# Attention, feed-forward and top-k on one core: the last query group's residual rows and second product in freed buffers, under a planner with new numbers

## The chip, the cores and the metric

One core of a Trainium2 chip. The number is device time in microseconds for the whole kernel; lower is better. TensorE is called PE here, VectorE DVE, ScalarE ACT, GpSimd POOL, and SyncE, which issues the DMAs, SP.

## The reference

`x` has shape (2, 4096, 256), float32. With C = 256:

```python
qkv = x @ w_attn + b_attn; q, k, v = split(qkv)
attn = softmax(q @ k.T / sqrt(C) + causal_mask)          # 4096 x 4096 per batch
x = layernorm(x + (attn @ v) @ w_proj + b_proj)
scores = x @ w_router;  top = top_k(scores, 3072)        # per batch of 4096 rows
y = x; y[top] = gelu(x[top] @ w_block)
out = layernorm(x + y)
```

## The kernel before

**Tiling.** The 4096 rows of a batch are cut into 8 groups of 512 queries, so there are 16 groups G = 0..15; G = 15 is the last. For each group the kernel goes over the key tiles of 128 rows that the mask leaves: 4 tiles on the diagonal (512, 384, 256 and 128 queries wide) and 4g full ones, 32 tiles for G = 15. Two tiles that follow each other are one softmax *unit* (128x1024); a diagonal tile is a unit by itself. Products are made with float32 halves: each is three matmuls (high by high, high by low, low by high).

**Steps of a group.** `scores` puts one tile's first product into one of two banks `sbank` (6 matmuls, L535), ACT copies it to a ring (L955), DVE keeps the running maximum (L992, L997). `row_max` transposes the maximum on PE (L1030), DVE reduces it (L1040 to L1047), PE spreads it again (L1053). Only then can the group's softmax begin: `softmax z` subtracts the maximum on DVE (L1066), `softmax exp` on ACT (L1073), `softmax hi` rounds to the high half on ACT (L1080; three buffers `parts`, so that unit u waits for PE to have finished unit u-3), `softmax lo` makes the low half on DVE (L1085). `values` is the second product, accumulated over all tiles of the group in two banks `obank` (L1134 to L1136, 6 matmuls of 512 columns for a full tile); its tiles of v come by DMA into six buffers (L1103). The first values tile of a group waits until the group before has been copied out of `obank` by ACT (`attention_out ot`, L1194, into `ot_sb`).

**After the second product.** PE turns the sums (L1225), DVE divides and adds the residual row `r` (`attention_out evac`, L1240, L1244), takes the statistics (L1251, L1256), POOL makes the root (`istd`, L1155 to L1160), ACT normalises (L1343). `r` is `xres[:, G % 2]`: rows of x loaded by SP (`attention_out load`, L1177) once the group two before has left that buffer, the bias added on POOL (`residual`, L1186). For G = 15 the router's product of these rows is taken ahead, on DVE (`last router`, L1373). The block product and gelu follow (`ffn`, L1477, L1542), the top-k search on DVE with counts on PE (`search`, L1668 to L1704; PE L1724), and the choice between the two outcomes (`final pick`, L1917). The last groups' work on ACT for both outcomes is `final own` and `final sums` (L1902, L1907), on rows that SP reloads during G = 15 (L1850, L1851).

**Order.** No engine's order is written by hand. Every step is put into a named stream of its engine; the function `merged` lists the waits and costs of each, `urgency` the longest way from it to the end, and `planned` walks through time and picks, engine by engine, the startable step with the smallest time rounded by `MARGIN_US`, then the largest urgency plus `PREFER_US`. `COSTS` and a few constants give its durations. The order it makes is what each engine executes, and an engine that waits for one step lets nothing behind it pass.

## Time and profile before

| | us |
|---|---|
| runs of the kernel | 958.93, 961.22, 964.9; median 961.22 |
| span of the profiled execution | 962.9 |
| PE busy in it | 934.3 |
| DVE / ACT / POOL busy | 791.0 / 637.6 / 303.6 |
| DMA queue 1, share of 16 engines | 51.5% |

The profiled execution has no other time than its span, which is 1.7 us above the median of the runs. Busy time of PE counts a matmul from its start to its modelled end, and matmuls overlap, so a full row of busy time still says nothing of the pace: that is read from the distance between two starts.

### The profile page before, as it was taken

The numbers are of one execution on the slowest core, as the hardware profiler recorded it, in microseconds if no ns is written. First come the engines' busy times: TensorE is split into PE (matmuls) and PEld (weight loads), VectorE is DVE, ScalarE is ACT, GpSimd is POOL, SyncE is SP. The second block draws the span as 40 slices with busy tenths as digits, with TensorE's granted clock in tenths as the row PEclk, the third lists the DMA queues.
The fourth block names the chain that finished last, engine by engine and source line by source line (L and its number), as shares of the span: only waits on it lengthen the run. The fifth ranks groups of instructions, "written<-read, shape, count | busy, mean of one in ns | idle before, by whom it ended". The sixth has DMA issues, their size and how long they took to land.

```text
span 962.9 us, 15643 instructions
## 1 busy us (share of the span) xinstructions
PE 934.3 (97%) x5018; PEld 799.2 (83%) x5018; DVE 791.0 (82%) x1494; ACT 637.6 (66%) x1009; POOL 303.6 (32%) x460
## 2 busy tenths in 40 slices
PE   9999999999999999999999999999999999998892
PEld 7889988888888888888889998888888888887671
DVE  5789886967976885699989898999899789489768
ACT  4467665764873776486757757586689577449794
POOL 3423231333220335414541253314212422131162
PEclk9999999999999999999999999999999999999996
DMA  6535344454364365488533633535769635347734
GB/s 212 166 114 171 113 141 122 120 158 126 101 184 116 102 187 155 132 255 277 175 109 94 199 108 110 164 102 172 247 223 295 212 106 153 99 144 241 264 128 175
DMA packets 89044, 155.84 MB, mean 162 GB/s; under 512 B 8442, under 2 KB 18300, under 8 KB 88964
## 3 DMA queue, kind: packets, MB, share of 16 engines
q1 hardware_dynamic: 88964, 154.85, 51.5%
q8 instruction: 41, 0.67, 0.3%
q14 instruction: 39, 0.32, 0.1%
HBM read 114.96 MB, written 39.86 MB: 161 GB/s over the span
## 4 chain that ended last, share of the span: by engine, by line
PE 93%; DVE 3%; DMA 1%; ACT 1%; issue 1%; DVEq 0%; POOL 0%; SPq 0%; ACTq 0%
PE sbank L535 38%; PE fbank L535 13%; PE obank L1134 11%; PE obank L1136 11%; PE obank L1135 10%; PE obank L1128 2%; PE obank L1130 2%; PE obank L1129 2%; DMA vs<-v_scratch 1%; PE fbank L1225 1%; PE mbank L1053 1%; PE mbank L1030 1%; DVE tail L1917 1%; PE fbank L1490 1%; DMA xraw<-xt 0%
## 5 line engine op out<-in xcount | busy, mean ns | idle before, releaser
L535 PE MATMUL sbank<-qT,xT 128*128 128x512 f32 (+2 forms) x1728 | 411.5, 378 | 0.2 <-issue 0.2
L535 PEld LDWEIGHTS sbank<-qT,xT 128*128 128x128 f32 x1728 | 304.9, 188 | 52.8 <-issue 0.6
L955 ACT COPY ring<-sbank 128x512 f32<-128x512 f32 (+3 forms) x286 | 156.2, 548 | 179.4 <-PE sbank L535 132.0
L1085 DVE TENSOR_TENSOR ring_lo<-ring,parts 128x1024 fp32r<-128x1024 f32 (+4 forms) x175 | 174.4, 1007 | 21.9 <-ACT parts L1080 21.3
L1134 PE MATMUL obank<-ring_lo,vs 128*128 128x512 f32 x476 | 182.5, 383 | 7.4 <-issue 3.5
L1136 PE MATMUL obank<-parts,vs 128*128 128x512 f32 x480 | 183.2, 382 | 0.0
L1135 PE MATMUL obank<-parts,vs 128*128 128x512 f32 x480 | 182.9, 381 | 0.0
L1080 ACT CAST parts<-ring 128x1024 fp32r<-128x1024 f32 (+4 forms) x175 | 144.8, 834 | 45.5 <-PE obank L1136 35.8
L1066 DVE TENSOR_TENSOR ring<-ring,mbank 128x1024 f32<-128x1024 f32 (+4 forms) x175 | 158.2, 944 | 7.3 <-PE mbank L1053 7.2
L1073 ACT ACTIVATE ring<-ring 128x1024 f32<-128x1024 f32 (+4 forms) x175 | 142.6, 842 | 21.6 <-DVE ring L1066 21.2
L997 DVE TENSOR_TENSOR runmax<-ring,runmax 128x1024 f32<-128x1024 f32 x84 | 106.6, 1269 | 59.3 <-ACT ring L955 58.6
L1134 PEld LDWEIGHTS obank<-ring_lo,vs 128*128 128x128 f32 x476 | 90.4, 190 | 25.1 <-issue 6.7
L1556 POOL TENSOR_TENSOR yb<-xres,yb 128x512 f32<-128x512 f32 x28 | 41.0, 1481 | 210.6 <-ACT yb L1542 80.1
L1136 PEld LDWEIGHTS obank<-parts,vs 128*128 128x128 f32 x480 | 90.9, 189 | 17.0
L1135 PEld LDWEIGHTS obank<-parts,vs 128*128 128x128 f32 x480 | 91.2, 190 | 16.1
L1186 POOL TENSOR_TENSOR xres<-xres,b_tot 128x512 f32<-128x512 f32 x32 | 49.0, 1554 | 67.5 <-DMA xres<-x 66.1
L839 POOL TENSOR_TENSOR xT<-xraw,xT 128x512 fp32r<-128x512 f32 x27 | 38.4, 1436 | 78.0 <-ACT xT L821 77.0
L1452 POOL TENSOR_TENSOR ot_sb<-ot_sb,yb 128x512 f32<-128x512 f32 x16 | 22.5, 1405 | 98.5 <-PE fbank L1225 80.6
L992 DVE TENSOR_TENSOR runmax<-ring,runmax 128x512 f32<-128x512 f32 (+3 forms) x74 | 44.9, 606 | 9.7 <-ACT ring L955 8.5
L535 PEld LDWEIGHTS fbank<-WV,xT 128*128 128x128 f32 x384 | 49.8, 191 | 2.3 <-issue 0.3
L535 PE MATMUL fbank<-WV,xT 128*128 128x256 f32 x384 | 51.2, 283 | 0.0
L535 PE MATMUL fbank<-xT,A 128*128 128x512 f32 x192 | 49.4, 393 | 0.2 <-POOL xT L839 0.2
(244 smaller groups left out, 1257.7 us busy)
## 6 DMA issues: line engine op xcount, KB each, us to landing
vs<-v_scratch SPq DMA_DIRECT2D x288, 256.0 KB, 2.9
v_scratch<-vnew SPq DMA_DIRECT2D x30, 512.0 KB, 3.1
xres<-x SPq DMA_DIRECT2D x16, 512.0 KB, 4.0
out<-tail SPq DMA_DIRECT2D x32, 256.0 KB, 2.8
x_scratch<-xres SPq DMA_DIRECT2D x14, 512.0 KB, 3.0
y_scratch<-yb SPq DMA_DIRECT2D x14, 512.0 KB, 4.1
tail<-x_scratch SPq DMA_DIRECT2D x28, 256.0 KB, 3.4
tail<-y_scratch SPq DMA_DIRECT2D x28, 256.0 KB, 4.0
```

The costliest lines, as they stand in the source:

```text
L535: mm = eng.matmul(o, lhs(lh, k), rhs(rh, k), start=n == 0, stop=n == len(todo) - 1)
L955: act.copy(slot(n)[:, c0:], sbank[n % NSS][:, c0:]).then_inc(a_copy, 1)
L992: dve.tensor_tensor(runmax[:, 0, c0:], slot(n)[:, c0:], runmax[:, 0, c0:], ALU.max).then_inc(v_max, 1)
L997: dve.tensor_tensor(runmax[:, :, :], slots(ns, 0), runmax[:, :, :], ALU.max).then_inc(v_max, 1)
L1066: dve.tensor_tensor(slots(ns, c0), slots(ns, c0), mbank[:, None, c0:].broadcast_to([P, len(ns), GQ - c0]), ALU.subtract).then_inc(v_z, 1)
L1073: act.activation(slots(ns, c0), slots(ns, c0), ACT.Exp, scale=SCALE).then_inc(a_exp, 1)
L1080: act.copy(hi_of(u), slots(ns, c0)).then_inc(a_hi, 1)
L1085: dve.tensor_tensor(slots_lo(ns, c0), slots(ns, c0), f32(hi_of(u)), ALU.subtract).then_inc(v_lo, 1)
L1134: pe.matmul(o, vh, lo_, start=i == 0, stop=False)
L1135: pe.matmul(o, vh, hi_, start=False, stop=False)
L1136: mm = pe.matmul(o, vl, hi_, start=False, stop=last)
L1186: pool.tensor_tensor(r[:, 2 * j:2 * j + 2], r[:, 2 * j:2 * j + 2], b_tot[:, None, :].broadcast_to([P, 2, C]), ALU.add).then_inc(g_xres, 1)
```

## The change

Four things are changed.

1. Rows of x for G = 15 are loaded into the end of `tail`, which is another name for the memory of x^T (`xT`), as soon as the last scores tile and the last projection are done (`p_s >= n_tiles` and the fill of v). Before, they went to `xres[:, 1]` and waited for group 13 to leave it.
2. The second product of G = 15 is accumulated in the two score banks `sbank`, not in `obank`, so its first tile waits for the last scores copy (`a_copy`), not for the copy of group 14. The banks of the late block products and of a small product (`last_ow`, now in `mbank`) are dealt anew.
3. `COSTS` and small per-instruction terms are set anew; a term is added that makes PE's operations cost 1.85 times as much for 3.5 us after it has been idle for over 1.3 us.
4. `PREFER_US` and `MARGIN_US` are replaced as a whole (by tables of 61 and 49 entries).

```diff
 COLD_US, COLD, COLD_STREAMS = 4.0, 1.85, ()
+IDLE_US, SLOW_US = 1.3, 3.5
...
-PREFER_US = {"ffn flo": 100, "final load": 100, "project vhi": 100, "ffn store": 100, "last chain": 60,
...
+PREFER_US = {"final_roots own": 462, "last": 416, "project qlo": 324, "project vhi": 309, "scores copy": 267,
...
-COSTS = {"pe": (.0, 1 / 2400, .2), "act": (.13, 1 / 1200, .14), "dve": (.09, 1 / 960, .12),
-         "pool": (.35, 1 / 460, .1), "sp": (.45, 0.0, 0.0)}
+COSTS = {"pe": (.0, 1 / 2383, .2), "act": (.075, 1 / 1200, .17), "dve": (.065, 1 / 960, .13),
+         "pool": (.1, 1 / 445, .18), "sp": (.45, 0.0, 0.0)}
...
-        time = r.time * (COLD if n in COLD_STREAMS or e == "pe" and when < COLD_US else 1.0)
+        if e == "pe" and when > 2 * COLD_US and when - free[e] > IDLE_US:
+            slow = when + SLOW_US
+        time = r.time * (COLD if n in COLD_STREAMS or e == "pe" and when < slow else 1.0)
...
-        bank_no[f] = (3, 4, 5, 3, 4, 5, 6, 3)[4 * (G - LATE) + 2 * j + (kind == "ff")]
+        bank_no[f] = (5, 6, 5, 3, 4, 5, 6, 3)[4 * (G - LATE) + 2 * j + (kind == "ff")]
...
-                if bank_no[f] == 6:
-                    eng.wait_ge(v_ot, CC)
-                    eng.wait_ge(v_ow, 1)
-                elif bank_no[f] == 5:
-                    eng.wait_ge(v_ot, 1)
+                if bank_no[f] >= 5:
+                    eng.wait_ge(a_ot, CC * (turned(LATE) + 1))
                 elif bank_no[f] >= 3:
-                    eng.wait_ge(a_copy, n_tiles)
+                    eng.wait_ge(v_ot, bank_no[f] - 2)
...
-        last_ow = obank[1][:, 0:QT]
+        last_ow = mbank[:, 160:160 + QT]
+
+        summed = lambda G: sbank if G == len(groups) - 1 else obank
...
                 if i == 0:
-                    if G and straight(G - 1):
+                    if G == len(groups) - 1:
+                        pe.wait_ge(a_copy, n_tiles)
+                    elif G and straight(G - 1):
                         pe.wait_ge(v_h, QT * G)
...
-                    o = obank[c][:, c0:]
+                    o = summed(G)[c][:, c0:]
...
             r = xres[:, G % 2]
+            if G == len(groups) - 1:
+                r = flat[:, (NUT - 2) * 512:NUT * 512].rearrange("p (t c) -> p t c", t=QT)
...
             def load(sp):
-                if G >= 2:
+                if G == len(groups) - 1:
+
+                    sp.wait_ge(p_s, n_tiles)
+                    filled(sp, ("v", G, 1))
+                elif G >= 2:
                     sp.wait_ge(st_x1[G % 2], 16 * (G // 2))
...
-                dve.tensor_copy(ot_sb[:, c, :], obank[c][:, :]).then_inc(v_ot, 1)
+                dve.tensor_copy(ot_sb[:, c, :], summed(G)[c][:, :]).then_inc(v_ot, 1)
```

The number of instructions on each engine stays the same; their order changes in every group. Three places in G = 15 follow. In the order lists the name left of the arrow is written, those right of it are read.

**PE, from the transpose of the last maximum to its spreading.** Before, the transpose is followed by the first half of group 13's block product (`fbank<-WB`, twelve matmuls, of which three rows are shown):

```order
L1136 MATMUL obank<-parts,vs 128x512
L1030 MATMUL mbank<-ident,runmax 128x128 x4
L535 MATMUL fbank<-WB,vnew_b 128x256 x2
L535 MATMUL fbank<-WB,x1p 128x256
...
L1053 MATMUL mbank<-ident,mcol 128x128 x4
```

Now it stands one values tile of group 14 earlier, and that tile comes after it:

```order
L1151 MATMUL obank<-parts,vs 128x512
L1043 MATMUL mbank<-ident,runmax 128x128 x4
L1149 MATMUL obank<-ring_lo,vs 128x512
L1150 MATMUL obank<-parts,vs 128x512
...
L1066 MATMUL mbank<-ident,mcol 128x128 x4
```

Two values tiles stood between the last projection and the transpose, now one; the block product's halves come after the spreading, the second one after the diagonal tiles of G = 15.

**DVE, the four router products of G = 15.** Before, they stand after fifteen units have had their z and ten their lo, behind the first evacuation of group 14:

```order
L1244 SCALAR_TENSOR_TENSOR xres<-fbank,rsum,xres 128x256 x2
L1066 TENSOR_TENSOR ring<-ring,mbank 128x1024
L1251 BN_STATS bnst<-xres 128x6 x2
L1085 TENSOR_TENSOR ring_lo<-ring,parts 128x1024
L1373 ISA runmax,mcol<-xres,wr 128x256
...
L1085 TENSOR_TENSOR ring_lo<-ring,parts 128x1024 x3
L1240 RECIPROCAL rsum<-fbank 128x2
```

Now three of them stand ahead of the first full lo, the fourth two lo's later, and they read `tail`:

```order
L1079 TENSOR_TENSOR ring<-ring,mbank 128x1024
L1098 TENSOR_TENSOR ring_lo<-ring,parts 128x128
L1394 ISA runmax,mcol<-tail,wr 128x256
...
L1098 TENSOR_TENSOR ring_lo<-ring,parts 128x1024 x2
L1394 ISA runmax,mcol<-tail,wr 128x256
L1394 ISA mcol 128x1
L1079 TENSOR_TENSOR ring<-ring,mbank 128x1024
```

**PE, the last values tiles and what follows.** Before, all values tiles are done before the first late transpose (`ident,tail`), the first three counts of the search (`cmp,ones_bf`) and the turn of G = 15 (`ident,ot_sb`):

```order
L1134 MATMUL obank<-late_lo,vs 128x512
L1135 MATMUL obank<-parts,vs 128x512
L1136 MATMUL obank<-parts,vs 128x512
L1490 MATMUL sbank<-ident,tail 128x128 x4
L1724 MATMUL fbank<-cmp,ones_bf 128x120 x3
L1225 MATMUL fbank<-ident,ot_sb 128x128 x8
```

Now the three counts stand ahead of the last seven values tiles, in the middle of a unit:

```order
L1745 MATMUL fbank<-cmp,ones_bf 128x120 x3
L1149 MATMUL sbank<-ring_lo,vs 128x512
...
L1149 MATMUL sbank<-late_lo,vs 128x512
L1150 MATMUL sbank<-parts,vs 128x512
L1151 MATMUL sbank<-parts,vs 128x512
L1511 MATMUL obank<-ident,tail 128x128 x4
L1246 MATMUL fbank<-ident,ot_sb 128x128 x8
```

What moved is the counts; the late transpose still stands ahead of the turn.

## Rows read from the trace of the kernel before

**Rows 1.** The page's head.

```profile
span 962.9 us, 15643 instructions
```

**Rows 2.** Busy time by stretch: stretch, length, engines with instruction counts, granted clock, DMA.

```profile
20.00:860.00 840.00, 838.95 (x4544) 725.08 (x4543) 698.61 (x1267) 555.04 (x873) 267.78 (x367) 1.00 0.51 155
860.00:926.00 66.00, 58.96 (x278) 48.56 (x278) 52.52 (x96) 51.17 (x77) 13.78 (x24) 0.95 0.75 251
926.00:963.00 37.00, 18.15 (x112) 12.05 (x111) 29.29 (x105) 23.58 (x51) 14.46 (x35) 0.77 0.31 114
```

**Rows 3.** PE's waits from 20 to 860 us: total, times, longest.

```profile
PE mbank L1053 <- DVE mcol L1047: 0.5, 2, 0.4
```

**Rows 4.** Timeline of PE around the stalls of G = 15.

```profile
863.16 0.60 PE L1030 MATMUL mbank<-ident,runmax 128*128 128x128 f32 x4
...
865.02 0.60 PE L1053 MATMUL mbank<-ident,mcol 128*128 128x128 f32 x4
...
871.42 0.47 PE L1134 MATMUL obank<-ring_lo,vs 128*128 128x512 f32 x1 [1.61 <-ACT ot_sb L1194]
...
876.97 0.47 PE L1134 MATMUL obank<-ring_lo,vs 128*128 128x512 f32 x1 [1.41 <-ACT parts L1080]
...
895.18 0.47 PE L1134 MATMUL obank<-ring_lo,vs 128*128 128x512 f32 x1 [0.50 <-DMA vs<-v_scratch]
...
900.33 0.47 PE L1134 MATMUL obank<-ring_lo,vs 128*128 128x512 f32 x1 [3.52 <-issue]
```

**Rows 5.** The chain that ended last, at full and at lower pace: start, us, what.

```profile
878.53 0.43 PE obank L1135
...
881.31 0.23 PE obank L1136
```

**Rows 6.** Busy time by stretch again (columns as in rows 2).

```profile
680.00:720.00 40.00, 40.00 (x210) 34.20 (x209) 38.27 (x78) 30.25 (x56) 7.33 (x14) 1.00 0.69 225
875.00:880.00 5.00, 3.59 (x13) 2.87 (x13) 5.00 (x5) 4.98 (x6) 0.00 (x0) 0.75 0.75 277
890.00:895.00 5.00, 4.69 (x21) 3.56 (x19) 1.53 (x3) 4.20 (x5) 0.55 (x1) 1.00 1.03 369
```

**Rows 7.** POOL, SP, DVE timelines: x rows of G = 15, DVE behind them.

```profile
886.15 0.38 SPq L1177 DMA_DIRECT2D xres<-x  x1
...
894.45 2.53 POOL L1186 TENSOR_TENSOR xres<-xres,b_tot 128x512 f32<-128x512 f32 x2 [10.47 <-DMA xres<-x]
...
895.77 1.49 DVE L1373 CUSTOM_DVE_ANT_0 runmax<-xres,wr 128x256 f32<-128x256 f32 x1 [4.25 <-POOL xres L1186]
...
897.44 0.43 DVE L1373 CUSTOM_DVE_ANT_0 runmax<-xres,wr 128x256 f32<-128x256 f32 x1 [0.17 <-DVE mcol L1373]
...
899.00 3.49 DVE L1085 TENSOR_TENSOR ring_lo<-ring,parts 128x1024 fp32r<-128x1024 f32 x3
```

**Rows 8.** Groups by shape from 865.6 to 918.2: busy, mean ns, idle before.

```profile
L1085 DVE TENSOR_TENSOR ring_lo<-ring,parts 128x1024 fp32r<-128x1024 f32 x13 | 15.8, 1239 | 1.4 <-ACT parts L1080 1.4
L1066 DVE TENSOR_TENSOR ring<-ring,mbank 128x1024 f32<-128x1024 f32 x13 | 15.4, 1212 | 0.0
L1073 ACT ACTIVATE ring<-ring 128x1024 f32<-128x1024 f32 x13 | 13.4, 1052 | 0.0
```

**Rows 9.** The same stretch as a whole (columns as in rows 2).

```profile
865.60:918.20 52.60, 45.56 (x201) 37.08 (x200) 44.58 (x69) 43.84 (x61) 8.93 (x10) 0.94 0.78 261
```

**Rows 10.** ACT's timeline at group 13's gelu.

```profile
879.16 1.28 ACT L1477 ACT_TABLE_LOAD   x1
880.45 1.57 ACT L1477 ACTIVATE yb<-fbank,fscale 128x256 f32<-128x256 f32 x4
```

**Rows 11.** Timelines after the last values tile: POOL, ACT, PE, DVE.

```profile
913.94 0.19 POOL L1155 TENSOR_SCALAR roots<-mv_h 128x4 f32<-128x4 f32 x1 [16.96 <-DVE mv_h L1256]
...
918.91 2.09 ACT L1343 ACTIVATE tail<-xres,rstd,rs_h 128x256 f32<-128x256 f32 x4
...
924.40 1.23 PE L1225 MATMUL fbank<-ident,ot_sb 128*128 128x128 f32 x8
...
949.35 9.85 DVE L1917 COPY_PREDICATED tail<-mbank,tail 128x512 f32<-128x512 uint32 x16
```

43 lines of the change are left out of this document (27 added, 16 removed).

## The prediction, as it was made before the run

> **What bounds the kernel now.** I read the busy times by stretch first [rows 2]. From 20 to 860 us PE is busy 838.95 of 840 us, and its only wait for another engine worth a row is 0.5 us, at the spreading of the maximum [rows 3]. Whatever the planner does to the order there, it can give back about a microsecond; it can only lose more. The last 103 us are different: from 860 to 926 PE is busy 58.96 of 66 us, and from 926 on 18.15 of 37, where the chain runs through DVE's search and the final choice.
>
> So I went through PE's timeline of group 15 [rows 4]. The spreading of the last maximum starts at 865.02, and the softmax of G = 15 can begin. PE then stalls four times: 1.61 us at 871.42 for ACT's copy of group 14 out of `obank`; 1.41 us at 876.97 for ACT's high half of the first full unit; 0.50 us at 895.18 for a tile of v; and 3.52 us at 900.33, where the row names only "issue". What that last one waits for is seen on the other engines [rows 7]: SP issues the rows of x for G = 15 at 886.15, POOL can add the bias at 894.45, 8.3 us later, and DVE, which has come to the router products, sits idle 4.25 us until 895.77 with the lo's of three units behind it. Those begin at 899.00, and PE starts 0.2 us after the first can be done. The chain of waits shows a second price of these stalls [rows 5]: at 878.53 a matmul of 512 columns takes 0.43 us from start to start, at 881.31 again 0.23. From 875 to 880 the granted clock is 0.75 on average, so part of it is at 1.2 GHz where the rest is at 2.4 GHz [rows 6]: the clock fell after PE had stood still for 1.61 and 1.41 us within 7 us, and again after the 3.52 us. Eight matmuls at 0.43 in place of 0.23 make 1.6 us each time, 3.2 us in all.
>
> The stalls and the clock sum to 1.61 + 1.41 + 0.50 + 3.52 + 3.2 = 10.2 us. The work of the other engines is what stands under that: from 865.6 to 918.2, from the first z to the last lo, DVE is busy 44.58 and ACT 43.84 of 52.6 us [rows 9]. Neither has more than 9 us to spare.
>
> **The change, part by part.** *Rows of x early.* The load moves on SP from 886.15 to just after the last scores tile and the last projection, about 860.5. Landing took 8.3 us before, with DMA queues at 1.03 busy between 890 and 895 [rows 6, 7]; taking all of that gives 868.8, and POOL's two additions of 1.27 us end at 871.4. The three router products now come about 871.2 on DVE, so their wait is nothing, or some tenths. Removed: 3.52 + 1.6 = 5.1 us. SP issues this load ahead of that of the late block weights, 0.4 us, which nobody needs for 50 us.
>
> *Second product in the score banks.* The first tile of G = 15 waits for the last scores copy, which is 5 us old by then. The wait of 1.61 us goes. ACT's two copies of group 14 no longer stand ahead of the first full units' work, so the following 1.41 us shrinks, and with it the clock's 1.6. Removed: up to 4.6 us. Next late there is DVE's lo of the first full unit (below).
>
> *The order at the transposes.* The last transpose moves up by one values tile: six matmuls 0.23 us apart [rows 5] make 1.4 us, from 863.16 to 861.8 [rows 4]. The running maximum allows it at about 862. Between transpose and spreading stands now that tile in place of twelve matmuls of half the width, a hundredth or two shorter, with DVE's reduction of 1.1 us behind it: at most 0.1 us of waiting. The softmax begins 1.1 us earlier, at 864.4. Gain 1.1.
>
> Gross: 10.2 + 1.1 = 11.3 us, and the last values matmul, which ended its row of work at 923.8, would be over at 912.5. That is PE with no wait at all. Three things are to be paid from it.
>
> *Routers in the ramp.* Three router products of 0.6 us (0.43, and 0.17 of gap [rows 7]) stand ahead of the lo that PE needs first. DVE's work up to there: z's and lo's of the diagonal, 2 x 1280 columns at 1.16 us per 1024 (3.49 for three lo's [rows 7]), 2.9 us; three full z's and a lo, 4.6; routers, 1.8; 9.3 us, plus some 0.3 of waiting for ACT, from 864.4: 874.0. PE comes there at 863.9 + 0.44 + 2.72 + 1.43 + 3.8 + 1.43 = 873.7 (spreading, two values tiles, half a block product, the diagonal tiles, the other half). Cost 0.3 to 0.8, taken 0.5, too short to lower the clock.
>
> *Three engines at their limit.* The stretch is to shrink from 52.6 to about 46 us, with 44 us of work on DVE (router products of group 14 come in, its feed-forward statistics go out) and 44 on ACT. A z costs 1.21, a lo 1.24, an exp 1.05 us [rows 8], so DVE needs some 2.3 us per unit where PE takes 2.72, and each evacuation, statistic or table load puts it behind. Two places are visible. Three counts of the search now stand in PE's order ahead of the last seven tiles, and wait for DVE's compare, which itself stands behind a lo, a statistic and four small steps: 0 to 1.3 us. Group 13's gelu moves behind eleven units' high halves, with a table load on each side (1.28 us [rows 10]). Bounds from 0 (all hidden) to 4 us (as much as DVE and ACT have left over now); I take 2, near the middle, because before they hid in slack that is now gone. DMA is the third: PE at full pace wants a tile of 256 KB each 1.36 us and two reloads of 256 KB every third tile, 322 GB/s, and 369 GB/s was moved between 890 and 895 [rows 6]. It is enough, with little over; the 0.50 us may stay or become 1. It lies in the 2.
>
> *Late transpose ahead of the turn.* It needs group 14 normalised. The chain from POOL's root at 913.94 to ACT's normalisation at 918.91 took 5.0 us [rows 11]. In the new order the statistics of group 14 are complete on DVE at about 909 or 910, so ACT could begin at 914 to 915, but stands behind ten passes of the final rows until about 915.6; two rows of tiles and the transpose make 917.0. The values would be over at 912.5 + 0.5 + 2 = 915.0 and the turn ready at 915.6. Cost 1.4, between 0 and 2.
>
> The turn began at 924.40 and begins at 917.0: **7.4 us** earlier.
>
> *The end.* From the turn to the end it took 962.9 - 924.4 = 38.5 us [rows 1, 11]. The instructions are the same. The statistics stand in other gaps of the search (three in one gap, 1.1 us where 0.7 fit: +0.4), and the last aggregation follows the choice's last step; POOL's 3 us for it and ACT's passes are needed by the last two of sixteen picks, 8 us into DVE's 9.85 [rows 11]. I take 0, between -1 and +1.
>
> *The start and the middle.* PE's order changes in every group, but the same matmuls fill it. Gain up to 1, loss up to 2 (four times the one wait of rows 3); I take 0. The new durations fit the rows better (DVE and ACT start to start), but PE did not wait, so that buys nothing there.
>
> **A table load by the skill.** The row shows 1.28 us from the load to gelu's start and no idle time before it. The Trainium skill ("ScalarE: Activation LUTs", What ACT_TABLE_LOAD costs) gives the load and then a drain of about 1.38 us, 2.66 in all, for every switch. By that, two switches amid ACT's full stretch would be some 2.8 us more than the row's, and the gain 4.6 instead of 7.4. The trace does not agree; I keep the row.
>
> **DVE and POOL side by side.** The first router product took 1.49 us where the others took 0.43, while POOL's addition ran until 897.0 [rows 7]; a DVE step can thus be held up to 1.06 us. In the new order POOL's two additions lie beside the first lo's of the ramp. The hold is in the bounds of the 2 us above. The Trainium skill ("SBUF — State Buffer", Who interferes with whom) says that a DVE instruction with two SBUF inputs contends with a POOL instruction that reads SBUF, and the one that comes second waits for all of the first. By that a hold could be as long as one addition, 1.29 us, twice; the row agrees in kind.
>
> **The rivals.** *All limits hold.* DVE, ACT and DMA keep up, the normalisation is in time, and only the 0.5 of the ramp is paid: 11.3 - 0.5 = 10.8 us, perhaps less a small wait. Time 950.4 to 951.5. For it: DVE is 97% busy from 680 to 720 (38.27 of 40) and PE does not wait [rows 6]. Against it: there PE had scores to put between.
>
> *The wait only moves.* The ramp or the middle of G = 15 still holds one stall of over 1.5 us with its 1.6 us of clock (late x rows, hi behind the gelu, the counts). Then 3.1 or more of the 7.4 is gone: 1 to 4.3 us gain, 957 to 960.
>
> *Slower, by the middle.* From 680 to 720 DVE has 1.7 us left in 40. If the new preferences put evacuations, statistics and routers ahead of a lo or a reduction that PE comes to, PE stands as in group 15: 1.6 to 3.5 us and 1.6 of clock, 3.2 to 5.1 each. Two such stalls eat the 7.4; with four over groups 3 to 14 the kernel is 5 to 13 us slower, 966 to 974. For it: every stream's preference changes at once. Against it: values tiles and scores tiles still alternate in the middle, and every transpose of a maximum keeps at least six full matmuls, 1.4 us, behind it.
>
> *No effect.* It would need DVE to be the bound of G = 15 already; at 44.58 of 52.6 with 4.25 us of waiting it is not.
>
> **How the numbers follow.** The profiled span is 962.9, the median of the runs 961.22. The gain is taken from the median: 961.2 - 7.4 = 953.8. Chances: the forecast (952 to 956) 0.55; all limits hold (below 951.6) 0.2; the wait only moves 0.17; slower or level by the middle 0.08. The range leaves out the last and a part of each end: 949 to 960. Runs of the kernel lie within 6 us of each other, so 1%, 9.6 us, is about what can be told from no change. Faster by over 1% means below 951.6: the second case and an edge of the first, 0.23. Slower by over 1%: 0.06. Within 1%: 0.71.
>
> **What would show it.** The first tile of G = 15 starts with no wait for `ot_sb`; no DVE idle time ahead of the router products; the clock 1.00 from 860 to the last values tile; the turn at 917 in place of 924.4 on a span whose first 860 us are alike; 38.5 us from there to the end. The forecast is wrong if PE's busy time from 20 to 860 falls by more than 2 us, if one stall in G = 15 is over 1.5 us, or if the turn waits for the late transpose by much more than 1.4.

## The result

The changed kernel takes 970.17 us (median of 4 runs, 967.69 to 972.97) against 962.55 for the kernel before on the same chip (4 runs): a ratio of 1.009, 95% interval 1.0058 to 1.0122. It is slower, where the prediction said 953.8 with a range that ended at 960. The profiled execution of the kernel after has a span of 971.2 us, that of before 962.9. Both were the longest of their first runs (972.97 us of 967.69 to 972.97, and 964.9 of 958.93 to 964.9), so the stretches below hold more stalls than the medians do.

The time splits at two points of PE's timeline: the last spreading of the maximum (G = 15) and the turn of G = 15's sums.

| | before | after | difference |
|---|---|---|---|
| start to last spreading | 865.0 | 880.3 | +15.3 |
| last spreading to turn | 59.4 | 50.9 | -8.5 |
| turn to end | 38.5 | 40.1 | +1.6 |

The stretch that the change aims at became shorter, in these two profiles by more than the 6.3 us forecast (59.4 to 53.1); against a second profile of the kernel before (e12 below) it is 3.9 us. The stretch in which "the same matmuls fill it" became 15.3 us longer.

The busy times by stretch after, in answer to [rows 2] (columns as there):

```profile
20.00:860.00 840.00, 829.40 (x4463) 713.55 (x4463) 692.84 (x1265) 544.51 (x862) 278.89 (x366) 1.00 0.48 154
860.00:926.00 66.00, 65.25 (x327) 54.70 (x326) 54.50 (x89) 49.94 (x74) 7.44 (x9) 1.00 0.73 244
926.00:971.00 45.00, 26.45 (x147) 18.81 (x145) 33.21 (x118) 30.45 (x63) 19.40 (x50) 0.79 0.37 134
```

Up to 860 us PE does 4463 matmuls where it did 4544. The busy time falls by only 9.55 us, since a matmul's modelled end covers short gaps; the count tells the lag better. From 860 to 926 it now stands still for 0.75 us instead of 7.04.

PE's waits in the whole trace, in answer to [rows 3] (total us, times, longest):

```profile
PE mbank L1043 <- DVE runmax L1005: 6.1, 5, 2.9
...
PE sbank L545 <- ACT ring L968: 1.8, 2, 1.3
PE fbank L545 <- DVE row_const L927: 1.4, 1, 1.4
...
PE sbank L1149 <- DMA vs<-v_scratch: 0.7, 1, 0.7
```

Before, the longest row of the middle was 0.5 us. Now PE waits before it transposes the running maximum (L1043), for a free score bank (L545, `sbank`), and before a projection (`fbank`). In the timeline of PE the five longest are these:

```profile
414.98 0.44 PE L1043 MATMUL mbank<-ident,runmax 128*128 128x128 f32 x2 [0.60 <-DVE runmax L1005]
418.44 0.47 PE L545 MATMUL fbank<-xT,A 128*128 128x512 f32 x1 [1.42 <-DVE row_const L927]
525.41 0.47 PE L1043 MATMUL mbank<-ident,runmax 128*128 128x128 f32 x1 [2.17 <-DVE runmax L1005]
727.68 0.50 PE L545 MATMUL sbank<-qT,xT 128*128 128x512 f32 x1 [1.29 <-ACT ring L968]
786.96 0.44 PE L1043 MATMUL mbank<-ident,runmax 128*128 128x128 f32 x2 [2.94 <-DVE runmax L1005]
...
878.45 0.60 PE L1043 MATMUL mbank<-ident,runmax 128*128 128x128 f32 x4
...
880.28 0.49 PE L1066 MATMUL mbank<-ident,mcol 128*128 128x128 f32 x3
...
892.70 0.47 PE L1149 MATMUL sbank<-ring_lo,vs 128*128 128x512 f32 x1 [0.68 <-DMA vs<-v_scratch]
...
931.17 0.38 PE L1246 MATMUL fbank<-ident,ot_sb 128*128 128x128 f32 x2
```

PE's waits from 20 to 860 us sum to 10.0 us here and to 1.0 before. After the waits of 2.17 and 2.94 us the granted clock fell: it is 0.57 on average from 525 to 529 us and 0.63 from 787 to 791, which costs some 1.6 us each, an estimate from the pace in [rows 5] (eight matmuls at 0.43 in place of 0.23). That makes 12.2 of the 15.3 us; the other 3 are in no row of waiting.

In G = 15 itself one wait of 0.68 us is left of the four in [rows 4]. Why DVE is late at 787 is seen on the other engines, DVE, SP, ACT and POOL:

```profile
783.61 0.98 DVE L1893 SCALAR_TENSOR_TENSOR tail<-tail,coef 128x256 f32<-128x256 f32 x2
785.55 0.75 DVE L1467 SCALAR_TENSOR_TENSOR yb<-yb,w_col 128x512 f32<-128x512 f32 x1 [0.97 <-DMA yb<-xt]
786.22 0.68 DVE L1005 TENSOR_TENSOR runmax<-ring,runmax 128x512 f32<-128x512 f32 x1
...
780.57 0.38 SPq L1459 DMA_DIRECT2D yb<-xt  x1
...
782.97 0.61 ACT L1885 ACTIVATE tail<-tail,coef 128x256 f32<-128x256 f32 x1 [3.77 <-DMA tail<-y_scratch]
...
781.95 1.07 POOL L1170 TENSOR_SCALAR roots<-mv_h 128x4 f32<-128x4 f32 x1 [9.07 <-DVE mv_h L1277]
783.10 1.34 POOL L1171 TENSOR_TENSOR roots<-roots,half 128x4 f32<-128x4 f32 x1
784.52 0.20 POOL L1172 TENSOR_TENSOR roots<-roots 128x4 f32<-128x4 f32 x1
...
786.45 0.51 POOL L1318 TENSOR_SCALAR rstd<-roots 128x4 f32<-128x4 f32 x1
```

The last running maximum of the group (L1005, at 786.22) stands in DVE's queue behind two steps of other work: a final result (L1893) and a scaling of rows (L1467), which waited 0.97 us for rows that SP had asked for at 780.57. The maximum could not have come before 784.53 in any case, since ACT copied its scores (L968, 783.97 to 784.53) behind a scaling that had waited 3.77 us for a reload. PE transposes as soon as L1005 is done. At 415 the step ahead is a score that waits for POOL:

```profile
414.12 0.18 DVE L1386 SCALAR_TENSOR_TENSOR score<-hw,rs_h 128x4 f32<-128x4 f32 x1 [1.25 <-POOL rs_h L1175]
414.23 0.69 DVE L1005 TENSOR_TENSOR runmax<-ring,runmax 128x512 f32<-128x512 f32 x1
```

At 525 POOL is behind it by way of ACT, whose score copy stands behind a rounding that waits for POOL's rows:

```profile
522.94 1.14 ACT L1477 CAST vnew_b<-ot_sb 128x512 fp32r<-128x512 f32 x2 [2.82 <-POOL ot_sb L1473]
...
524.67 0.69 DVE L1005 TENSOR_TENSOR runmax<-ring,runmax 128x512 f32<-128x512 f32 x1 [2.90 <-ACT ring L968]
```

At 787 POOL's root chain ends at 786.96, when PE's transpose starts, but nothing that PE waited for there waited for the chain. What the two times show is the slack: in the kernel before the chain of the same group had ended at 770.40, and the transposes came 5.0 us later:

```profile
770.21 0.19 POOL L1297 TENSOR_SCALAR rstd<-roots 128x4 f32<-128x4 f32 x1
...
775.40 0.38 PE L1030 MATMUL mbank<-ident,runmax 128*128 128x128 f32 x2
```

### The profile page after: what moved, and what is told of

It reads as the page before. It is cut to its first block, busy times and chain, and to the rows that moved or that the text cites. A ratio compares the mean times of both kernels' runs of the same rounds, so it can differ in the third digit from the quotient of the medians.

```text
span 971.2 us, 15640 instructions
## 1 busy us (share of the span) xinstructions
PE 940.1 (97%) x5018; PEld 800.8 (82%) x5018; DVE 790.4 (81%) x1494; ACT 632.9 (65%) x1009; POOL 313.8 (32%) x460
## 4 chain that ended last, share of the span: by engine, by line
PE 74%; DVE 9%; DMA 6%; POOL 5%; issue 3%; ACT 2%; SPq 0%; DVEq 0%; ACTq 0%; POOLq 0%
PE sbank L545 29%; PE fbank L545 11%; PE obank L1149 7%; PE obank L1150 7%; PE obank L1151 7%; DVE ring L1079 2%; POOL xT L852 2%; DMA xraw<-xt 2%; DMA out<-tail 2%; PE obank L1143 1%; PE obank L1145 1%; PE obank L1144 1%; PE sbank L1149 1%; PE sbank L1151 1%; PE sbank L1150 1%
## 5 line engine op out<-in xcount | busy, mean ns | idle before, releaser
L545 PE MATMUL sbank<-qT,xT 128*128 128x512 f32 (+2 forms) x1728 | 409.8, 378 | 2.6 <-ACT ring L968 1.8
L545 PEld LDWEIGHTS sbank<-qT,xT 128*128 128x128 f32 x1728 | 307.4, 189 | 59.3 <-ACT ring L968 5.3
L968 ACT COPY ring<-sbank 128x512 f32<-128x512 f32 (+3 forms) x286 | 156.7, 551 | 156.1 <-PE sbank L545 116.0
L1098 DVE TENSOR_TENSOR ring_lo<-ring,parts 128x1024 fp32r<-128x1024 f32 (+4 forms) x175 | 184.2, 1061 | 21.7 <-ACT parts L1093 20.6
L1010 DVE TENSOR_TENSOR runmax<-ring,runmax 128x1024 f32<-128x1024 f32 x84 | 110.1, 1311 | 72.7 <-ACT ring L968 71.8
L1149 PE MATMUL obank<-ring_lo,vs 128*128 128x512 f32 (+3 forms) x416 | 159.9, 384 | 0.2 <-ACT ot_sb L1215 0.2
L1150 PE MATMUL obank<-parts,vs 128*128 128x512 f32 (+3 forms) x416 | 157.9, 380 | 0.0
L1151 PE MATMUL obank<-parts,vs 128*128 128x512 f32 (+3 forms) x416 | 157.9, 380 | 0.0
L1577 POOL TENSOR_TENSOR yb<-xres,yb 128x512 f32<-128x512 f32 x28 | 36.9, 1338 | 186.3 <-ACT yb L1498 107.4
L1149 PEld LDWEIGHTS obank<-ring_lo,vs 128*128 128x128 f32 x416 | 78.6, 189 | 15.1 <-issue 1.6
L1151 PEld LDWEIGHTS obank<-parts,vs 128*128 128x128 f32 x416 | 78.6, 189 | 14.8
L1150 PEld LDWEIGHTS obank<-parts,vs 128*128 128x128 f32 x416 | 78.8, 189 | 13.4
L1207 POOL TENSOR_TENSOR xres<-xres,b_tot 128x512 f32<-128x512 f32 x30 | 45.9, 1553 | 64.9 <-DMA xres<-x 62.5
L852 POOL TENSOR_TENSOR xT<-xraw,xT 128x512 fp32r<-128x512 f32 x27 | 41.5, 1555 | 49.9 <-ACT xT L834 48.8
L545 PE MATMUL fbank<-WV,xT 128*128 128x256 f32 x384 | 51.5, 284 | 0.1
L545 PEld LDWEIGHTS fbank<-WV,xT 128*128 128x128 f32 x384 | 49.6, 191 | 2.1 <-DVE WV L748 0.3
L545 PE MATMUL fbank<-xT,A 128*128 128x512 f32 x192 | 49.8, 395 | 1.6 <-DVE row_const L927 1.4
L1005 DVE TENSOR_TENSOR runmax<-ring,runmax 128x512 f32<-128x512 f32 (+3 forms) x74 | 38.7, 523 | 12.3 <-ACT ring L968 10.6
```

The costliest lines, as they stand in the source:

```text
L545: mm = eng.matmul(o, lhs(lh, k), rhs(rh, k), start=n == 0, stop=n == len(todo) - 1)
L852: pool.tensor_tensor(xT[:, 1, k, cols], raw_of(G)[:, k, :], f32(xT[:, 0, k, cols]), ALU.subtract).then_inc(g_xlo, 1)
L968: act.copy(slot(n)[:, c0:], sbank[n % NSS][:, c0:]).then_inc(a_copy, 1)
L1010: dve.tensor_tensor(runmax[:, :, :], slots(ns, 0), runmax[:, :, :], ALU.max).then_inc(v_max, 1)
L1098: dve.tensor_tensor(slots_lo(ns, c0), slots(ns, c0), f32(hi_of(u)), ALU.subtract).then_inc(v_lo, 1)
L1149: pe.matmul(o, vh, lo_, start=i == 0, stop=False)
```

## The experiments

A, the order that the new numbers give puts steps that still wait ahead of what PE comes to. B, the new banks and buffers cost it. C, DVE and POOL disturb each other more than before. Each experiment was compared with the kernel before on one chip; each ran 4 to 12 times. Where two experiments are compared, it is by the difference of their ratios, 0.1% being 1 us. "Spreading" and "turn" are of G = 15 in the one profiled execution, which can be a long or a short one: that of the changed kernel and that of e8 were the longest of their runs, those of e1, e2, e7 and e13 the shortest.

| kernel | median us | ratio to before (95%) | spreading | turn |
|---|---|---|---|---|
| after | 970.17 | 1.009 (1.0058 to 1.0122) | 880.3 | 931.2 |
| e1_tables | 982.05 | 1.0208 (1.0183 to 1.0233) | 879.3 | 937.7 |
| e2_structure | 981.9 | 1.0207 (1.018 to 1.0233) | 864.3 | 930.9 |
| e3_new_costs | 985.23 | 1.0242 (1.0218 to 1.0267) | 872.2 | 939.0 |
| e4_switch | 977.61 | 1.0159 (1.0132 to 1.0186) | 864.6 | 926.2 |
| e5_banks | 963.08 | 1.0018 (1.0003 to 1.0034) | 865.6 | 921.5 |
| e6_rows | 959.95 | 0.9987 (0.9972 to 1.0001) | 866.6 | 921.3 |
| e7_splice | 958.14 | 0.9968 (0.9955 to 0.9981) | 865.2 | 916.3 |
| e8_moves | 970.88 | 1.0102 (1.008 to 1.0124) | 882.6 | 933.4 |
| e9_short_chain | 966.51 | 1.0052 (1.0033 to 1.0071) | 873.0 | 922.9 |
| e10_cut | 967.28 | 1.0065 (1.0042 to 1.0088) | 876.3 | 926.4 |
| e11_late_rows | 962.43 | 1.0015 (1.0003 to 1.0027) | 865.2 | 921.7 |
| e12_again | 961.49 | 1.001 (0.9992 to 1.0028) | 867.0 | 921.8 |
| e13_behind | 968.83 | 1.0095 (1.008 to 1.0111) | 876.9 | 926.8 |
| e14_splice_short | 957.48 | 0.9968 (0.9954 to 0.9983) | 865.5 | 917.2 |
| e15_behind_short | 966.87 | 1.0076 (1.006 to 1.0091) | 876.2 | 927.2 |

**e1_tables and e2_structure: numbers or structure.** The first is the kernel before with all the new numbers, the second the changed kernel with the old ones (`slow` never begins, its small terms are the old ones too).

```diff
 # e1: before.  e2: after, with + and - exchanged
-PREFER_US = {"ffn flo": 100, ...        COSTS = {..., "pool": (.35, 1 / 460, .1), ...
+PREFER_US = {"final_roots own": 462, ...  COSTS = {..., "pool": (.1, 1 / 445, .18), ...
-MARGIN_US = {"attention_out router": 3, ...
+MARGIN_US = {"final sums": 5, ...
```

> The kernel before with only the planner's numbers of the change (preferences, margins, durations, price on idle TensorE); rows of x and sum banks of group 15 stay as they were. TensorE's order is then that of the changed kernel up to about 780 us. Theory A, the new numbers put steps that still wait ahead of the last running maximum and the score copies: the spreading of the last maximum at 877 to 882 instead of 865, with the stalls of about 1.6, 2.3 and 3.1 us at 418, 525 and 787 us, and a time of 972 to 980. Theory B, the new banks and the early load cost it: spreading at 864 to 867, time 959 to 964.

> The changed kernel with all of the planner's numbers as before: only the early rows of x, the sums in the score banks and the banks around them are left of the change. Theory A: spreading of the last maximum at 864 to 866, and from there to the turn of group 15 50 to 54 us instead of 59.4, so 953 to 958. Theory B: spreading at 876 or later, time 968 or more.

For the stretch to the last spreading A holds and B falls: 879.3 with the new numbers in the old structure, 864.3 with the old numbers in the new structure. The times miss theory A's ranges, by 2 us in e1 and by 24 in e2, though not for theory B's reason: what was not expected is the rest of e2: from the spreading to the turn it takes 66.6 us where 50 to 54 were expected, and the end 48.5. What became late is seen on POOL:

```profile
863.89 2.53 POOL L1197 TENSOR_TENSOR tail<-tail,b_tot 128x512 f32<-128x512 f32 x2 [31.40 <-DMA tail<-x]
867.31 1.34 POOL L1463 TENSOR_TENSOR ot_sb<-ot_sb,yb 128x512 f32<-128x512 f32 x1 [0.88 <-PE fbank L1236]
897.06 1.30 POOL L1463 TENSOR_TENSOR ot_sb<-ot_sb,yb 128x512 f32<-128x512 f32 x1 [28.41 <-DVE yb L1457]
908.72 0.19 POOL L1160 TENSOR_SCALAR roots<-mv_h 128x4 f32<-128x4 f32 x1 [10.36 <-DVE mv_h L1267]
```

In e2's order the bias addition of G = 15 (L1197), now of the early rows of x, stands ahead of group 13's feed-forward rows and root. POOL stands 31.40 us in front of the load, and group 13's root starts at 908.72; group 14's, which began at 913.94 before [rows 11], starts at 931.71. Gelu, statistics and normalisation of both groups fall behind the last values tile. POOL's standing is not the only thing that moved: PE's turn of group 13 comes at 866.12, where it came at 845.45 before, and its root waits for DVE's statistics, done at 908.63. So the whole order around group 13 is late, and which step of the plan began it was not tested. The order that the old numbers make does not fit the new structure.

**e3_new_costs and e4_switch: which numbers.** e3 keeps the new durations with the old preferences and margins; e4 the old durations, and the new preferences only from 850 us of the plan on.

```diff
 # e3: after, with before's PREFER_US and MARGIN_US
 # e4: after, with all of before's numbers, and in planned():
+            prefer, margin = ((LATE_PREFER_US, LATE_MARGIN_US) if max(free.values()) > 850 else
+                              (PREFER_US, MARGIN_US))
```

> The changed kernel with the old preferences and margins, but the new durations and the price on idle TensorE. Splits theory A. A1, the preferences and margins do the harm: spreading at 864 to 868, time 953 to 960. A2, the durations do it, since GpSimd's small steps are now taken as 0.3 us where they were 0.45 and the chains through it look ready too early: spreading at 874 or later, time 964 to 972.

> The changed kernel with the old durations throughout, and the old preferences and margins until the plan is at 850 us, the new ones from there on. If the gain in group 15 and the loss before it are independent, the spreading comes at 865 and the turn 50.9 us later, at 916: 952 to 955. If the new preferences give nothing over the old ones in group 15 it equals the kernel with the structure alone, within 1.5 us.

Both missed, since e2's fault in group 13 is in e4's order too (turn at 926.2), and e3 adds 7.2 us before the spreading (872.2, between its two cases) to losses at the end. Against e2 (864.3), from which it differs by the durations and the price on an idle PE alone, its spreading is 7.9 us later, by one profile each: those numbers by themselves lose time in the middle. Every change of one table gives another order everywhere, so tables cannot be tested one by one. From here on the order was written out for each engine and no longer planned:

```diff
+ORDER = {
+    "pe": ("prepare*4,proj*6,scores*7,proj*3,scores,proj*2,row_max,scores*2,row_max,proj,scores*4,...
...
+    orders = {e: written(e, todo) for e in orders}
     return {e: [todo[e][n][i][0] for n, i in order] for e, order in orders.items()}, times
```

**e5_banks, e6_rows, e7_splice: the gain, part by part.** e5 is the new structure in exactly the old order. e6 moves one operation. e7 takes the order of before up to 857 us of its plan and the changed kernel's behind it.

```diff
 # e6: order of SP
-..., "values load" (274), "attention_out load" (15), "values load" (275), ...
+..., "attention_out load" (15), "late load" (0), ..., "values load" (274), "values load" (275), ...
 # e7: all engines
+order = [op of before's order if planned before 857] + [rest, in the order of after]
```

> The changed kernel's program in exactly the order of the kernel before on all five engines (the order is written out, no planning): of the change only the sums of group 15 in the score banks are in effect, with the new buffer for the rows of x, which are still loaded at the old place. Theory S, the structure itself is sound and what lost 18 us in the kernel with the structure alone was the plan made with the old numbers: the spreading of the last maximum at 865, the wait of 1.61 us for the copies of group 14 gone and up to 3 us behind it, time 957 to 961. Theory B', the new banks or buffers themselves cost: 965 or more.

> As the kernel with the new banks and the old order, with one step moved: the load of the rows of x of group 15 on the DMA-issuing engine, from amid the loads of v tiles to just ahead of the late block weights. If the wait of 4.25 us of VectorE for these rows is what held TensorE for 3.52 us and lowered its clock for 1.6, it is 3.5 to 5.1 us faster than the one without the move: 952 to 957. If other steps of VectorE are late next, as the prediction's 2 us of three engines at their limit say, it is 1.5 to 3 us.

> The changed kernel's program in a written order: that of the kernel before up to 857 us of its plan, and the rest in the changed kernel's order. Theory A, the loss is only in the middle's order and the gain only in group 15's: spreading at 865, the turn of group 15 at 916, and 40 us to the end, 954 to 957 us. If the two hang together (group 15 ran well only because group 13's and 14's steps had been done early in the middle), the turn is at 920 or later and the time 959 or more.

e5 takes 0.18% longer than before (0.03 to 0.34%), between its two cases: the structure costs little, and the banks alone gain nothing. The wait moved. This is PE in e5, beside [rows 4]:

```profile
875.25 0.30 PE L1451 MATMUL sbank<-ring_lo,vs 128*128 128x128 f32 x1 [1.75 <-issue]
...
877.52 0.77 PE L1451 MATMUL sbank<-ring_lo,vs 128*128 128x512 f32 x1 [1.41 <-ACT parts L1395]
...
898.62 0.47 PE L1451 MATMUL sbank<-ring_lo,vs 128*128 128x512 f32 x1 [2.15 <-ACT parts L1395]
```

No wait for `ot_sb`, and instead 1.75 and 1.41 us in the next units. The second is put down to ACT's high half (`parts`), as in [rows 4], but these are DVE's low halves. In the kernel before and in e5:

```profile
875.65 1.22 DVE L1085 TENSOR_TENSOR ring_lo<-ring,parts 128x1024 fp32r<-128x1024 f32 x1
...
876.21 1.21 DVE L1400 TENSOR_TENSOR ring_lo<-ring,parts 128x1024 fp32r<-128x1024 f32 x1
```

They end at 876.87 and 877.42, and PE's matmul, which reads `ring_lo`, starts 0.10 us behind each (876.97 and 877.52), while ACT's first full high half was done by 875.33 in the kernel before. DVE's order is the same in both kernels, with a step of z ahead of each low half, so a wait for it did not shrink when ACT's copies moved.

e6 is 0.31% faster than e5, 3.0 us, the upper end of its second case, the third stall gone. e7 is another 0.19% faster, 1.8 us (958.14 against 959.95 in 12 runs each on one chip), and beats both kernels: 0.32% under the one before. Its time is above its expectation (954 to 957), but spreading and turn came at 865.2 and 916.3 as theory A has it, and its profiled execution, the shortest of the twelve, took 957.09. **The changed kernel is 1.22%, 11.7 us, slower than e7, which differs from it by the order before the softmax of group 15 alone.** That is the loss in the middle; by the two intervals it lies between some 8 and 15 us. e7 keeps the old place of the last transpose and its spreading too, so the third part of the predicted gain, 1.1 us, is not in it.

**e8_moves: six operations.** In the changed kernel's order, on DVE and ACT:

```diff
-score 5, running maximum 94
+running maximum 94, score 5
-ffn fhi 14, 15, score copy 167, ..., score copy 168
+score copy 167, 168, ffn fhi 14, 15
-final result 15, ffn scale 13, running maximum 170
+running maximum 170, final result 15, ffn scale 13
```

and `project vhi` 15 ahead of a normalisation, score copy 255 ahead of a final scaling.

> The changed kernel with six operations moved in its plan, at the four longest stalls of the middle: at 415 and 787 us the last running maximum ahead of a score, a final result and a scaling of rows that wait for GpSimd or a DMA; ScalarE's score copies at 523 and 783 us ahead of casts and a scaling that wait; at 415 us the high half of v ahead of a normalisation. Theory A: those stalls (0.76, 1.59, 2.33, 3.11 us) and the clock behind two of them (1.6 each) go, the spreading of the last maximum comes 8 to 11 us earlier, at 869 to 872, time 959 to 962. Theory C, VectorE is late as a whole because GpSimd contends with it more: the stalls stay, in whole or moved by a tile, and the time is 967 or more.

Nothing was gained: 970.88 us (1.0102), in the range of theory C. The waits at the transposes shrank, and came back at the spreading behind them:

```profile
787.53 0.33 PE L1054 MATMUL mbank<-ident,runmax 128*128 128x128 f32 x1 [0.29 <-DVE runmax L1016]
...
792.85 0.32 PE L1077 MATMUL mbank<-ident,mcol 128*128 128x128 f32 x1 [1.87 <-DVE mcol L1071]
```

The steps that wait now stand between the last running maximum and the reduction. A as I had put it, a step misplaced by one position, falls; C was not told apart from a lateness of the whole order.

**e9_short_chain, e14_splice_short: GpSimd's root.** The planner reckons nine steps of 0.359 us, seven waits of 0.1 and 0.8 for the power with the old `COSTS`, 4.73 us; with the new ones 9 x 0.109 + 7 x 0.18 + 0.8 = 3.04. From the first step to the scale, the eighth, that is 4.37 and 2.93. In the traces the same eight steps take 3.04 to 5.89 us in 15 groups before (median 4.46) and 3.47 to 5.76 after (median 4.41).

```diff
-            link(pool.tensor_tensor(root, v, half[:, 0:rs.shape[-1]], ALU.pow))
-            link(pool.tensor_tensor(tmp, root, root, ALU.mult))
-            link(pool.tensor_tensor(tmp, tmp, v, ALU.mult))
-            link(pool.tensor_scalar(tmp, tmp, -0.5, 1.5, ALU.mult, ALU.add))
-            pool.tensor_tensor(rs, root, tmp, ALU.mult).then_inc(done, 1)
+            pool.tensor_tensor(rs, v, half[:, 0:rs.shape[-1]], ALU.pow).then_inc(done, 1)
```

> The changed kernel in its own order, written out, but the inverse square root on GpSimd is two steps (the power, without the refinement by one Newton step) instead of six; the refinement is left out. In the changed kernel this chain takes 3.5 to 5.8 us (median 4.4) from the variance to the scale, where its plan reckons with 3.04. Theory A2, the plan's order is bad because the chain is later than planned: with some 1.3 to 2 us less of chain the stalls of the middle at 415, 418 and 525 us shrink by that much each, the one at 787 little (it waits for a DMA), the spreading comes 4 to 8 us earlier and the time is 962 to 966. If the order as such is bad (steps of other groups ahead of the running maximum whatever their inputs), it is 968 or more.

> The spliced kernel with the refinement of the inverse square root left out, as in the changed kernel with the short chain: a control. That one was 3.7 us faster than the changed kernel. If the chain through GpSimd hurts only where the new order stands it ahead of what TensorE comes to, this is within 1 us of the spliced kernel up to the last spreading (865 against 865.2) and at most 1.8 us faster in all, by the end: 956.3 to 958.5. If a shorter chain helps any order, the spreading comes 3 us or more earlier, time 955 or less.

With the chain at 2.91 us (median), what the new plan reckons with, the changed kernel's order gives 1.0052 instead of 1.009: 3.7 us, though the two intervals overlap, and the time is half a microsecond above the range expected. In the profiled executions the spreading comes at 873.0 instead of 880.3; but that of e9 is one of its shorter ones (963.99, its clock did not fall in the middle) and the other the longest of its kernel, so 7.3 us is too much. The wait at 525 shrinks from 2.17 to 0.32 us and the one at 787 from 2.94 to 1.45. The control does not move: 0.9968 again, spreading 865.5. So no gain from the shorter chain is seen in the order of e7, and a probable one in the changed kernel's.

**e10_cut: do the losses add up?**

```diff
-order = [op of before's order if planned before 857] + [rest, in the order of after]
+order = [op of before's order if planned before 628] + [rest, in the order of after]
```

> Order of the kernel before up to 628 us of its plan, from there the changed kernel's order. Theory A, each stall belongs to its place in the order and they add up: the changed kernel lost 2.7 us up to 632 us and 12.6 from there to the last spreading, so the spreading comes at 877 to 878 and the time is 969 to 972. If the loss needs the whole order (a lateness that is built up from the start and carried on), the spreading comes at 872 or earlier, 965 or less.

Spreading at 876.3, and 0.97%, 9.3 us, above e7. So about 2.4 of the 11.7 us are lost before 628 and the rest behind it; the stalls belong to their places, at 783 again with 2.44 us of waiting for the running maximum. Its time is 1.7 us under the range of theory A and 2.3 above the other case.

**e11_late_rows, e12_again: the size of the gain.** e11 is e7 with the load and the four router products put back; e12 has no edit.

```diff
 # e11, on e7: SP, DVE
-"attention_out load" (15), "late load" (0), ...
+..., "values load" (274), "attention_out load" (15), "values load" (275), ...
-"last router" (0, 1, 2), "softmax lo" (162), ...
+..., "last router" (0 to 3), "softmax lo" (168), ...
```

> The written order of the spliced kernel with two things put back: the load of the rows of x of group 15 goes out amid the v tiles (ahead of the load of tile 275), and the four router products stand on VectorE ahead of the low half of unit 168, as before. The term of the prediction for the early rows, 3.5 of waiting and 1.6 of clock, is right if this is 3.5 to 5.1 us slower than the spliced kernel, 961.5 to 963.5; if other work hides half of it, 959.5 to 961.

> The kernel before, unchanged, for a second profile of it. The profiled execution that the prediction was worked out from took 964.9 us where 29 runs have their median at 961.5. If it was only a slow one, this profile shows the same stalls in group 15, of 1.6, 1.4, 0.5 and 3.5 us, with a turn at 921 to 925; if the stalls themselves change from run to run, one of them is shorter by 1 us or more, and the turn lies 3 us earlier.

e11 is 0.47%, 4.5 us, slower than e7, within the 3.5 to 5.1 of its first case. Its trace, DVE and PE:

```profile
890.02 1.50 DVE L1698 CUSTOM_DVE_ANT_0 runmax<-tail,wr 128x256 f32<-128x256 f32 x1 [1.42 <-POOL tail L1511]
...
891.71 1.22 DVE L1698 CUSTOM_DVE_ANT_0 runmax<-tail,wr 128x256 f32<-128x256 f32 x1 [0.17 <-DVE mcol L1698]
...
893.11 1.23 DVE L1698 CUSTOM_DVE_ANT_0 runmax<-tail,wr 128x256 f32<-128x256 f32 x1 [0.17 <-DVE mcol L1698]
...
896.19 0.77 PE L1453 MATMUL sbank<-ring_lo,vs 128*128 128x512 f32 x1 [4.85 <-ACT parts L1397]
```

The second profile of the kernel before, unchanged, has the same first two waits (1.61 us at 873.40) but not the same fourth. POOL and PE, beside [rows 4, 7]:

```profile
892.58 2.55 POOL L1186 TENSOR_TENSOR xres<-xres,b_tot 128x512 f32<-128x512 f32 x2 [6.61 <-DMA xres<-x]
...
898.48 0.47 PE L1134 MATMUL obank<-ring_lo,vs 128*128 128x512 f32 x1 [2.02 <-ACT parts L1080]
```

SP issued at 886.55, so the rows took 6.0 us instead of 8.3, PE waited 2.02 instead of 3.52, and from spreading to turn it was 54.8 us instead of 59.4. The shorter wait makes 1.5 of these 4.6 us. The rest is the clock, which did not fall in this execution, though the first two waits were the same. Here is the second of them, and the busy times around both, first in the first profile and then in this one:

```profile
878.94 0.47 PE L1134 MATMUL obank<-ring_lo,vs 128*128 128x512 f32 x1 [1.41 <-ACT parts L1080]
...
871.00:882.00 11.00, 9.17 (x39) 7.78 (x40) 11.00 (x12) 10.97 (x16) 0.57 (x1) 0.84 0.62 212
...
873.00:884.00 11.00, 9.19 (x46) 7.91 (x47) 11.00 (x11) 10.97 (x16) 0.59 (x1) 1.00 0.69 237
```

From 898 to 903 us, behind the wait of 2.02, the clock is 1.00 as well; behind that of 3.52, from 900 to 905, it was 0.66.

**e13_behind, e15_behind_short: the waiting steps behind the reduction.** In the changed kernel's order the steps of e8 go behind the reduction of the maximum, with three router products, a low half and a search step; score copies, a high half and the copies of the sums go ahead of the gelu at 725 us. e15 adds the short chain (its refinement is left out here too).

```diff
 # DVE at 787 (the others alike)
-final result 15, ffn scale 13, running maximum 170, router 49 to 51, row_max reduce 14
+running maximum 170, row_max reduce 14, final result 15, ffn scale 13, router 49 to 51
 # ACT at 725
-gelu 11, score copy 235, 236, softmax hi 130, ot 12, 13
+score copy 235, 236, softmax hi 130, ot 12, 13, gelu 11
```

> The changed kernel in its own order, written out, with the steps that waited or filled in moved behind the reduction of the maximum instead of only behind the last running maximum: at 415 us a score and a low half, at 525 us a score and a search step, at 787 us a final result, a scaling of rows and three router products on VectorE; on ScalarE the score copies and high halves ahead of casts, of a scaling and of the gelu at 725 us. Those stalls hold 9.2 us and the clock 3.2. If the place of these steps in the order is the cause, the spreading of the last maximum comes 6 to 10 us earlier, at 870 to 874, time 960 to 964. If the stalls only move, as in the kernel with six moves, it comes within 2 us of 880 and the time is 968 to 971.

> The moves behind the reduction and the short chain together, in the changed kernel's order. If both are parts of the same loss the gains overlap: 958 to 963, spreading at 868 to 872. If they are independent and each is whole, it reaches the spliced kernel, 958 us or less.

The spreading of e13 comes 3.4 us earlier than the changed kernel's in the profiled executions, its shortest against the other's longest, but the ratio, 1.0095, is the same as 1.009. The five waits are gone or short, except the one for the score bank, 1.80 us at 730, and others stand behind them:

```profile
787.74 0.39 PE L838 MATMUL fbank<-WB,vnew_b 128*128 128x256 f32 x1 [1.12 <-DVE x1p L1774]
...
791.95 0.50 PE L838 MATMUL fbank<-xT,A 128*128 128x512 f32 x1 [1.06 <-POOL xT L1145]
...
799.76 0.30 PE L1442 MATMUL obank<-ring_lo,vs 128*128 128x128 f32 x1 [1.17 <-ACT parts L1386]
```

e15 is no better than the short chain alone (1.0076 and 1.0052), and outside both its cases. Moving single steps on DVE and ACT does not mend the order.

SP's order was never tested, and there the traces differ most. Its waits for a store of `out` to land, with the following loads behind it, from 20 to 860 us, in the changed kernel and in the kernel before:

```profile
SPq L1869 <- DMA out<-tail: 53.3, 14, 5.9
...
SPq L1848 <- DMA out<-tail: 12.1, 9, 2.8
```

In e7 they sum to 12.2 us. One of the changed kernel's, 4.9 us, ends at 779.67, just ahead of the two loads for which ACT and DVE are late at 787.

## Why the prediction was wrong

**The step that failed** is "The start and the middle", where the prediction took 0 with "gain up to 1, loss up to 2 (four times the one wait of rows 3)". It measured 15.3 us in the two profiles and 11.7 us by the runs of e7. The bound was taken from a wait of the old order, and says nothing of an order made with other numbers. What the runs showed in its place are PE's waits for the last running maximum, for score banks and for a projection, which with two small ones are 10.0 us, with the clock lowered behind two of them. The prediction had set its own sign for it, PE's busy time from 20 to 860 falling by more than 2 us: it fell by 9.55.

**The rival "Slower, by the middle"** named the mechanism, several stalls between groups 3 and 14, two of them with a lowered clock, and 966 to 974 us; the time is 970.17. It was given 0.08. What I set against it, that each transpose keeps six full matmuls behind it, protects only the wait between transpose and spreading. The waits came ahead of the transpose, where the last running maximum has no such cover. And DVE, at 38.27 of 40 us in [rows 6], was read in that rival as a reason for the loss, and had no part in the term's bound of 2 us.

**"The new durations fit the rows better, but PE did not wait, so that buys nothing"** left out that a fit can cost. They fit an undisturbed GpSimd: 2.93 us for a chain whose median is 4.4. The old 4.37 is near the disturbed value. With it the chain ended 5.0 us ahead of the transposes at 775, with the new one at the same moment at 787; that the duration made this difference is argued. e3 against e2 shows that the new durations and the idle price cost 7.9 us up to the spreading, and the share of the late chain is some 3.7 us (e9 against the changed kernel, with overlapping intervals; e14 as the control).

**Group 15.** From the spreading to the turn the prediction gave 53.1 us (863.9 to 917.0); it took 50.9 in the changed kernel and 51.1 in e7. The turn of e7, 916.3 against 917.0, and its span, 955.3 against 962.9 - 7.4 = 955.5, look as predicted, but that is in part luck: it is e7's shortest execution against a count from a long one of the kernel before, without the 1.1 us of the transposes, and some of the parts are off:
- Rows of x early, 5.1 us: 4.5 (e11) in the new order, 3.0 (e6) in the old.
- The clock, 3.2 of these 10.2 us: it fell in one of two profiles of the kernel before with the same first two waits, so it is a cost of some executions and not of all.
- Banks, "up to 4.6 us": nothing by themselves (e5, "the wait only moves"), since the wait of 1.41 us was read as one for ACT and was one for DVE's low half. The new order of group 15, in which the copies of group 14 and block products go elsewhere in the ramp, made 1.8 of it (e7 against e6).
- The transposes one values tile earlier, 1.1: from the start of the last projection (875.62 and 858.97) to the spreading it is 4.66 us in the changed kernel and 6.05 before, 1.4 less. What it is worth in the time was not tested.
- Routers in the ramp and three engines at their limit, 0.5 and 2: the changed kernel keeps one wait worth a row between spreading and turn, the 0.68 for a tile of v; in e7 PE waits 0.80 us at 869.4 and up to 0.39 at three more places. That is 0.7 and 1.7 us where 2.5 were taken.
- Late transpose ahead of the turn, 1.4: nothing. Neither kernel has a row of waiting ahead of it (930.74 in the changed kernel, 915.84 in e7).

**"The gain is taken from the median"** is a second step that failed, by 3 to 4 us. The profiled execution took 964.9 us, the highest of the first runs; 29 runs of the same kernel had their median at 961.47. Part of it lay in the very stalls that were to be removed and in the clock behind them: in the second profile, with the rows landing after 6.0 us instead of 8.3 and no fall of the clock, the turn is 4.6 us nearer to the spreading (that execution lost 2.0 us before the spreading and 1.6 behind the turn instead). So e7 is worth 0.32%, 3.1 us, and not 7.4.

**The end**, predicted 0 between -1 and +1: 40.1 us after, 39.0 in e7, and 40.1 also in the kernel before when profiled again; nothing of the 1.6 is the change's.

**A table load by the Trainium skill** ("ScalarE: Activation LUTs", What ACT_TABLE_LOAD costs): at 903.80 in the changed kernel the load again takes 1.28 us and gelu starts 1.29 us behind its start, with no drain. The row was right to keep.

**DVE and POOL side by side.** The traces show the hold in both directions: router products of 0.42 us took 1.50, 1.22 and 1.23 beside POOL's additions, and POOL's small steps, 0.20 us alone, took 1.07 in the chain at 781.95. The Trainium skill ("SBUF — State Buffer", Who interferes with whom) has the one that comes second wait for the whole of the first; a hold of 0.8 to 1.08 us under an addition of 1.28 agrees in kind. From 20 to 860 us the low halves of 1024 columns take 1347 ns instead of 1274 and POOL's additions for x^T 1566 instead of 1442:

```profile
L1098 DVE TENSOR_TENSOR ring_lo<-ring,parts 128x1024 fp32r<-128x1024 f32 x96 | 128.8, 1347 | 13.3 <-ACT parts L1093 12.9
...
L852 POOL TENSOR_TENSOR xT<-xraw,xT 128x512 fp32r<-128x512 f32 x26 | 40.2, 1566 | 48.8 <-ACT xT L834 48.8
```

**What stays open.** That the middle's order costs about 11.7 us is shown, that some 3.7 of them need the late chain is likely. The other 8 us are not settled: the waits name reloads that land late, a gelu with its table load ahead of score copies, and steps of two groups before; but moving these (e8, e13, e15) only moved the waits, and neither SP's waits for its stores nor theory C was tested by itself. Each could be a cause of the lateness or its companion.

## What to carry to other kernels

Where a change hands the order of all engines to new numbers, "PE does not wait now" is no bound for what it will do: price the order from the slack that the dependents of slow chains have now, and look for who loses it. Give a planner the durations that a step takes beside its neighbours, not alone; no run here tried that directly, but the order made with the undisturbed ones probably gained when the chain was shortened to them. Before a gain is taken from one profile, see where that execution lies among the runs: the stalls to be removed may be what made it slow, and the best part of a change (here the rows of x loaded early and group 15's order, with the old order before it) may be worth keeping without the rest.
